# Attention passes of a graph network on one core: TensorE fetches one K|V row in 14 by one-hots kept in DRAM, and the weighed rows live in one buffer that is scanned in place

## The reference

```python
alpha = jnp.sum(q[dst] * k[src], axis=-1) * SCALE      # the third adds edge_bias[edge_type]
m = jax.ops.segment_max(alpha, dst, num_segments=N)
a = jnp.exp(alpha - m[dst])
denom = jax.ops.segment_sum(a, dst, num_segments=N)
out = jax.ops.segment_sum(v[src] * (a / denom[dst])[:, :, None], dst, num_segments=N)
```

## Time and profile before

| | us |
|---|---|
| median of 3 runs without a profile | 5822.36 (5817.04 to 5822.9) |
| the profiled execution (one), its span | 6562.2 |
| pass 2, 3 and 4 in it: from the first row fetch to the last | 1080, 1080, 1083 |
| pass 5 and 6 in it: from the first row fetch to the last | 1003, 992 |

### The profile page before, as it was taken

How to read it: one execution, slowest core, us unless ns; L and a number is a source line. 1 busy time by engine, 2 the same in 40 slices (tenths; PEclk the granted TensorE clock), 3 DMA queues, 4 the chain that set the end, 5 groups by cost and what they waited for, 6 DMA issues and landing times.

```text
span 6562.2 us, 44574 instructions
## 1 busy us (share of the span) xinstructions
PE 2310.6 (35%) x14635; PEld 1387.8 (21%) x14635; DVE 4507.3 (69%) x5353; ACT 2519.0 (38%) x3136; POOL 3944.3 (60%) x3878
## 2 busy tenths in 40 slices
PE   4988400000020000000100000046877783778886
PEld 2775300000000000000000000023444441444443
DVE  7978587777767777776787777764655653656654
ACT  2330144444424444443344444433444442444443
POOL 1001377777747777775677777656665555566664
PEclk8998755555555555555555555567888895889887
DMA  2233354444434444443454444412333322333332
GB/s 64 83 136 135 110 163 152 153 147 146 152 117 151 157 148 147 152 148 113 134 160 152 147 148 146 142 46 86 102 110 101 101 95 73 102 110 109 98 103 84
DMA packets 257146, 807.72 MB, mean 123 GB/s; under 512 B 72026, under 2 KB 108938, under 8 KB 253123
## 3 DMA queue, kind: packets, MB, share of 16 engines
q0 software_dynamic: 162688, 416.67, 22.2%
q1 hardware_dynamic: 94279, 389.14, 16.2%
HBM read 473.23 MB, written 332.30 MB: 123 GB/s over the span
## 4 chain that ended last, share of the span: by engine, by line
POOL 38%; PE 26%; issue 22%; DVE 8%; ACT 2%; another core or an unknown queue 2%; DMA 1%; SPq 0%; DVEq 0%; POOLq 0%; ACTq 0%
POOL arena L2316 38%; PE pair_ps L1864 20%; PE pair_ps L1966 3%; DVE outs L917 2%; ACT outs L1702 1%; PE banks_ps L1830 1%; PE banks_ps L1942 1%; DVE outs L995 1%; PE pair_ps L1873 0%; DVE bn_st L700 0%; DVE H L1048 0%; ACT arena L1680 0%; PE pair_ps L1982 0%; PE banks_ps L1807 0%
## 5 line engine op out<-in xcount | busy, mean ns | idle before, releaser
L2316 POOL DMA_INDIRECT arena<-table,src_i x3596 | 3684.6, 1025 | 1549.8 <-issue 1134.4
L1842 PE MATMUL pair_ps<-ident,tails 128*128 128x128 f32 x9 | 2.7, 439 | 3331.7 <-DVE tails L1246 3331.7
L1864 PE MATMUL pair_ps<-bias,arena 128*128 128x384 bf16 x4050 | 803.9, 348 | 279.9 <-issue 239.9
L1092 DVE TENSOR_TENSOR pair_ps<-pair_ps,arena 128x1792 f32<-128x1792 f32 x168 | 341.5, 2033 | 764.7 <-DMA arena<-table,src_i 589.1
L1864 PE MATMUL pair_ps<-work,arena 128*128 128x384 bf16 x4050 | 760.5, 338 | 206.4 <-issue 204.8
L995 DVE TENSOR_TENSOR_SCAN outs<-arena,banks_ps 128x1920 f32<-128x1920 f32 x112 | 465.2, 4153 | 494.3 <-ACT banks_ps L1688 446.2
L1842 PEld LDWEIGHTS pair_ps<-ident,tails 128*128 128x128 f32 x9 | 1.5, 213 | 3334.0 <-DVE tails L1246 3334.0
L1140 DVE TENSOR_TENSOR_SCAN work<-work,banks_ps 128x1920 f32<-128x1920 f32 x168 | 697.7, 4153 | 5.8
L1562 ACT ACTIVATE LD<-DE 128x112 f32<-128x112 f32 x168 | 49.8, 296 | 1440.9 <-issue 571.3
L1864 PEld LDWEIGHTS pair_ps<-bias,arena 128*128 128x128 bf16 x4050 | 406.9, 102 | 661.6 <-issue 452.8
L1582 ACT COPY outs<-work 128x1792 f32<-128x1792 f32 x171 | 541.0, 3165 | 0.0
(11 more groups left out here) (321 smaller groups left out, 4353.4 us busy)
## 6 DMA issues: line engine op xcount, KB each, us to landing
rows_att<-outs SPq DMA_DIRECT2D x165, 1008.0 KB
rows_plain<-outs SPq DMA_DIRECT2D x110, 896.0 KB
arena<-table,src_i POOLq DMA_INDIRECT x3596
kept_counts<-arena SPq DMA_DIRECT2D x15, 2000.0 KB, 6.4
bias<-sources SPq DMA_DIRECT2D x108, 192.0 KB
arena<-kept_counts SPq DMA_DIRECT2D x10, 2000.0 KB, 8.3
outs<-kept_counts SPq DMA_DIRECT2D x5, 2000.0 KB, 8.0
table<-arena SPq DMA_DIRECT2D x18, 512.0 KB, 3.0
```

Of the source, the lines that this page charges most:

```text
L1092: chain(v.tensor_tensor(prod, prod, ring[:, s, :, 0:D], ALU.mult))
L1864: ins = pe.matmul(picked_ps[g % 2], parts3[:, a, t, :], hots_made[g % 2][:, :, t, :], start=t == a == 0, stop=t == NB - 1 and a == 2)
L2316: pool.indirect_dma_start(dst, None, tab, bass.IndirectOffsetOnAxis(ap=idx, axis=0))\
```

## The change

Four things change in the attention passes.

1. From group 12 on POOL fetches 13 rows of a group, and PE makes the fourteenth: 25 tiles of the table times a one-hot of 125 x 128 bytes (fp8), for three bf16 parts of the table that add up to the f32 row, so 75 matmuls of 256 columns (`pick_table_row`). ACT copies the result from PSUM to the ring (`lay_pick`), and the product with K waits for that.
2. The table comes back from DRAM to SBUF at the start of each pass in 13 units of 2 tiles (`load_unit`), and DVE takes each apart into three bf16 parts with three casts and two subtractions (`split_units`), 5 units in group 0, 2 in group 1, and one each in groups 2 to 7. The parts stand where the edge bias and a node buffer stood; so the edge bias is stored to DRAM once and comes back by the group in pass 4.
3. The one-hots of the 44 groups are made once, ahead of the passes: SP clears 44 blocks of DRAM in the cells pass (`clear_hots`, 5 after each store of counts), POOL writes the ones by 44 indirect transfers of single bytes, and SP loads 400 KB per group in each pass (`load_hots`).
4. `OS` is one buffer, and the PSUM tile `msg` goes: the product of V with the weights writes `OS`, and the scan runs in place on it. The product waits until ACT has copied out the rows of the group before (it was two groups before). Clearing at the start of a pass gets shorter.

The core of the diff:

```diff
             def part_a(k, g):
...
+                split_units(k, g)
                 v.wait_ge(s_land[s], landed(k, g))
+                if row_picks(k, g):
+                    v.wait_ge(s_row_laid, row_pick(k, g) + 1)
                 chain(v.tensor_tensor(prod, prod, ring[:, s, :, 0:D], ALU.mult))
...
+            def split_units(k, g):
...
+                    for a in range(3):
+                        part = row_parts(k, a, t0, t1)
+                        ins = v.tensor_copy(part, rest)
+                        if a < 2:
+                            step(ins)
+                            step(v.tensor_tensor(rest, rest, part, ALU.subtract))
...
             def part_b(k, g):
...
-                chain(v.tensor_tensor(by_edge(msg).rearrange("p j (h c) -> p j h c", c=CH), vals, wts,
+                if g:
+                    v.wait_ge(s_rows, rows_base[k] + 2 * g)
+                chain(v.tensor_tensor(by_edge(OS).rearrange("p j (h c) -> p j h c", c=CH), vals, wts,
                                       ALU.mult))
-                if g >= 2:
-                    v.wait_ge(s_rows, rows_base[k] + 2 * (g - 1))
-                chain(v.tensor_tensor_scan(OS[b], dB[b], msg, 0.0, ALU.mult, ALU.add))
+                chain(v.tensor_tensor_scan(OS, dB[b], OS, 0.0, ALU.mult, ALU.add))
...
             def clear_carries(k, name):
-                step(v.memset(banks_ps[:, :], 0.0))
-                step(v.memset(work[:, 0:4 * GS], 0.0), f"cleared{k}")
+                step(v.memset(LA, 0.0))
+                step(v.memset(work[:, 0:3 * GS], 0.0), f"cleared{k}")
...
+            def lay_pick(k, s, b, n):
+                act.wait_ge(s_row_pick, n + 1)
+                act.copy(ring[:, s, GROUP - 1, :], row_ps[b]).then_inc(s_row_laid, 1)
...
             def near_pass(k):
...
                     lay_rows(k, g % RING, g % 2, g, stored(k, g))
+                    if ROW_FROM <= g + RING < GROUPS:
+                        lay_pick(k, g % RING, (g + RING) % 2, row_pick(k, g + RING))
...
+            def pick_table_row(k, g, it=None):
...
+                for t in range(NB):
+                    for a in range(3):
+                        ins = pe.matmul(row_ps[g % 2], hot[0:NX, t, :], row_parts(k, a, t, t + 1)[0:NX, 0, :],
+                                        start=t == a == 0, stop=t == NB - 1 and a == 2)
+                ins.then_inc(s_row_pick, 1)
...
             def store_rows(k):
...
+                        if ROW_FROM + 2 <= g + 5 < GROUPS:
+                            load_hots(k, g + 5)
...
+            def load_hots(k, g):
...
+                if g - 2 >= ROW_FROM:
+                    sp.wait_ge(s_row_pick, row_pick(k, g - 2) + 1)
...
-                        for j in range(GROUP):
+                        for j in range(GROUP - row_picks(k, g)):
                             fetch(ring[:, s, j, :], table[k], src_i[:, first + j:first + j + 1], s_land[s])
...
+            for h in range(ROW_PICKS):
+                pool.indirect_dma_start(row_hots, bass.IndirectOffsetOnAxis(ap=hot_at[:, h:h + 1], axis=0),
+                                        one_8[:, 0:1], None).then_inc(s_ones, 16)
```

More of the change, by code:

```diff
@@ L61 @@
 SHARE = 7
+ROW_FROM = 12
+ROW_PICKS = GROUPS - ROW_FROM
+UNIT = 2
+UNITS = -(-25 // UNIT)
+UNIT_BUF = 3
+UNITS_AT = (5, 2, 1, 1, 1, 1, 1, 1)
+HOT_ROWS = 1 << 12
+CLEAR_EACH = 5
 QROWS = SHARE + 1
@@ L350, in gnn_kernel, with row_parts @@
         columns_turned = work[0:PICKED // 2, columns_at:columns_at + 2 * P].rearrange("p (a e) -> p a e", a=2)
+        rows_in = {k: (KEEP[:, :] if k == 4 else H[:, :, :].rearrange("p i f -> p (i f)")).bitcast(BF16)
+                   .rearrange("p (i f) -> p i f", f=2 * D) for k in range(PASSES) if KINDS[k] == ATT}
+        more_rows = bias_flat[:, 0:(2 * NB - 1) * D].bitcast(BF16).rearrange("p (i f) -> p i f", f=2 * D)
+        odd_row = work[:, ODD_AT:ODD_AT + D].bitcast(BF16).rearrange("p (i f) -> p i f", f=2 * D)
+        def row_parts(k, a, t0, t1):
+            if a == 0:
+                return rows_in[k][:, t0:t1, :]
+            if a == 2 and t1 == NB:
+                return odd_row[:, t0 - (NB - 1):1, :]
+            return more_rows[:, (a - 1) * NB + t0:(a - 1) * NB + t1, :]
         HOT = NB * P // 2
@@ L1095, in part_a @@
                 if k == 4:
-                    chain(v.tensor_tensor(scores, scores, bias[:, first:first + GROUP, :], ALU.add))
+                    v.wait_ge(s_bias_in[g % BIAS_BUF], 16 * (g // BIAS_BUF + 1))
+                    chain(v.tensor_tensor(scores, scores, bias_in[:, g % BIAS_BUF, :, :], ALU.add))
                 chain(v.tensor_tensor_scan(flat(MS[:, s, :, :]), flat(fences[:, b, :, :]), flat(UA[:, b, 1, :, :]), 0.0,
@@ L1104, in part_a @@
                 assert n == A_STEPS[k]
+            def split_units(k, g):
+                if g >= len(UNITS_AT):
+                    return
+                if k == 2 and g == 0:
+                    v.wait_ge(s_bias_kept, 16)
+                for i in range(sum(UNITS_AT[:g]), sum(UNITS_AT[:g + 1])):
+                    t0, t1 = i * UNIT, min((i + 1) * UNIT, NB)
+                    rest = units[:, i % UNIT_BUF, 0:t1 - t0, :]
+                    v.wait_ge(s_unit[i % UNIT_BUF], units_loaded(k, i))
+                    for a in range(3):
[4 more added lines that the diff above has]
+                            step(v.tensor_tensor(rest, rest, part, ALU.subtract))
+                    ins.then_inc(s_split, 1)
             def move_on(k, g):
@@ L1650, in far_pass @@
                 whole_sixes = (GROUPS - RING) // SIX
-                with act.Fori(0, whole_sixes) as it:
+                for g in range(ROW_FROM):
+                    far_group(g % RING, g % OUT, g, stored(k, g))
+                with act.Fori(ROW_FROM // SIX, whole_sixes) as it:
                     for i in range(SIX):
@@ L2172, in store_rows @@
                 dst = rows[KINDS[k]].rearrange("(p t) f -> p (t f)", t=STEPS)
+                if KINDS[k] == ATT:
+                    for b in range(NBLK - QBUF, NBLK):
+                        sp.wait_ge(s_kvq[b % QBUF], kvq_count(k, b))
+                    if k == 4:
+                        for g in range(BIAS_BUF):
+                            load_bias(g)
+                    for i in range(sum(UNITS_AT[:3])):
+                        load_unit(k, i)
                 if k in PICKS:
@@ L2327, in far_group @@
                 pool.nop(nofuse=True)
-                for j in range(GROUP):
+                for j in range(GROUP - (not isinstance(g, int) or row_picks(k, g))):
                     fetch(ring[:, s, j, :], table[k], near_idx[:, s, 0, j:j + 1], s_land[s])
@@ L2350, in run_pass @@
                 with pool.If(slow > 0):
-                    for g in range(RING):
-                        far_group(k, g, g)
-                    with pool.Fori(1, LOOPS) as it:
+                    for g in range(ROW_FROM):
+                        far_group(k, g % RING, g)
+                    with pool.Fori(ROW_FROM // RING, LOOPS) as it:
                         for s in range(RING):
```

129 lines of the change are left out of this document (114 added, 15 removed).

## The result

The changed kernel takes 6226.55 us (median of 4 runs, 6218.81 to 6230.12) where the kernel before takes 5822.31: 1.070 times as long (95% interval 1.068 to 1.071), so 404 us slower. 6250 was forecast, 428 slower, with a range of 5980 to 6350.

A forecast was written before the change was run, and what follows sets the result against it. POOL's row fetches, one every 1.25 us, were taken to bound the attention groups. 5822 - 165 (fewer fetches) + 539 (scan's hold) + 47 (L1113's hold) + 9 (splits) = 6252, said as 6250 us, range 5980 to 6350.

The forecast's parts named there:

- POOL as the bound, 1.25 us per fetch: Attention groups: POOL starts a row fetch every 1.25 us, 17.5 us per group, and DVE has about 2.7 us to spare.
- The longer profiled execution: Profile of the kernel before: 740 us longer than its runs, because recording stretches it; the changed kernel's profile should stretch likewise.
- 132 fetches fewer, -165 us: Attention passes: 44 groups in 3 passes lose one 1.25 us fetch each, 165 us less.
- The scan in place, +539 us: Long DVE scan, now with two SBUF inputs: holds one fetch 3.33 us in each of 162 groups, 539 us, bounds 445 to 640.
- The window move behind it, +47 us: L1113, after the scan: holds a later fetch 0.34 us in 139 groups, 47 us, bounds nothing to 80.
- The splits, +9 us: DVE's 78 subtractions that take the table apart: 0.55 of them catch a fetch, 9 us, bounds nothing to 40.
- What should cost nothing: PE's picks (8.1 to 16.3 us each), ACT's copies, loads, clears and ones: all hidden behind other work, no time added.
- The sum: Whole kernel: 5822 - 165 + 539 + 47 + 9 = 6252, said as 6250 us, 7% slower; this case reaches 6110 to 6350.
- Groups: Attention passes: groups of about 21 us before the twelfth and 19.6 to 20 after it.
- The scan that holds nothing (5660): Rival at the fetch starting inside the scan: it takes 0.95 us, so the gain stands alone, about 5660 us; 8%.
- The stall that is real (6000): Rival: 2.10 us fetches late in a pass also happen without the profiler, and the hold hides them; 6000 us, 9%.
- the late picked row (6700): Rival: load, pick and copy run one after another, 23 us per group; DVE waits 3.4 us in 132 groups; 6700, 8%.

The follow-up runs named there:

- the run with 8 pieces: The changed kernel with the in-place scan cut into 8 scans of 16 channels each, all inputs still in SBUF: 5831.12 us, 1.002 times before.

## Why the prediction was right, step by step

**POOL as the bound, 1.25 us per fetch.** Right. The kernel before, profiled again, has passes of 1000, 993 and 1008 us; 790 transfers behind the first at 1.25 us each are 987.5. (The working counted 783 fetches and left out the windows, which before and after have alike.)

**The longer profiled execution.** The half on which the sum rests was right: its 740 us were of that execution. That the five passes seemed to hold 750 us of excess, so all of it, was luck: against the second profile they held 660, and 90 lay outside of them. The other half, "a profile of the changed kernel should be longer than its own runs in the same way", was wrong: its span is 6217.1 us and its runs take 6219 to 6230. Such stretching is no property of the kernel; the second profile told.

**132 fetches fewer, -165 us.** Right; the version with the scan's input back in PSUM is 165 us below before, and its passes lose about that beyond the smaller holds.

**The scan in place, +539 us.** Right in kind, place and count (162), and 19 us too large: 3.21 us each make 520. The working put every fetch 0.67 us into the scan and its end 0.80 behind it. In the trace the held ones start 0.05 to 1.29 us into it, 0.76 on average, and end 0.75 behind it. That the 0.67 of the kernel before still served is in part luck: the product's extra 1.2 us, which the working didn't have, moves the scan by nearly a whole step of 1.25 us from fetch to fetch. The lower bound was 445, the upper 640.

**The window move behind it, +47 us.** Measured 60.4 us in the changed kernel. The same instruction cost 24.1 in before, which the working didn't take off, so the change adds 36.

**The splits, +9 us.** Measured 4 us, with the casts, which the working didn't count.

**What should cost nothing.** It did: PE's picks take about 10.7 us each by the windows of pass 3 below (107.00 us for 750 matmuls, ten picks), inside the 8.1 to 16.3 forecast and far within a group of 20; ACT's copy takes 0.36 us, and DVE never waits for it. Two things were missed. The product into SBUF became 1.2 us longer, which was hidden by DVE's wait for rows but weighs in the run with 8 pieces. And outside the attention passes' fetches the profiled execution is 15 us longer than the second one of before, 12 of it between passes 2 and 3 and between 3 and 4 (91.6 and 112.2 us against 85.7 and 106.2). About 7 of these 12 lie ahead of the pass's last scan: it ends 24.0 us after the start of the pass's last fetch, where it was 20.5. The other 5 lie behind it. The version with the input in PSUM has both parts as well, the scan in place alone only 2 us of them, so they don't come from the scan's inputs; which of the other parts of the change makes them wasn't tried.

**The sum.** All other fetches together took 9 us beyond 0.947 in before and 3 in the changed kernel, so -6. Then -165 + 520 + 36 + 4 - 6 + 15 = 404, which is what was measured. The sum on record has 430: its three holds are 35 us too large, and it lacks the 6 us less and the 15 us more. Its range was drawn too narrowly: with its own bounds of 80 for the move and 40 for the splits, the top is 6417 and not 6350.

**Groups.** About 21 us before the twelfth and 19.6 to 20 after were forecast. From scan to scan it is 21.4, 21.4 and 21.6 us on average in the first eleven groups of the three passes, and 20.0, 20.0 and 20.1 after them.

**The rivals.** The scan that holds nothing (5660) is refuted by 162 fetches, and by the two experiments that put the time at 6376 and 5652 with that one input moved. The Trainium skill's page "SBUF — State Buffer", section "Who interferes with whom", has the rule that a VectorE instruction with two SBUF inputs contends with a GpSimd instruction that reads SBUF, and an inference that making descriptors needs only the write side. The trace agrees with the rule for the issue of these transfers, which read their row numbers from SBUF, whatever the output: 520 us. The inference, taken to mean that such an instruction leaves them alone, doesn't hold for them; no run here has a transfer of POOL without row numbers. The stall that is real (6000) falls with the second profile of before, the late picked row (6700) with DVE's waits, none of which is for it.

## What to carry to other kernels

Where POOL issues indirect transfers without a break, look at the operands of each long VectorE instruction beside them: when a buffer moves from PSUM to SBUF and leaves the instruction no input in PSUM, a transfer that starts inside it stands until its end, though the instruction itself is no slower. Price it per transfer, as the rest of the instruction less what the issue covers anyway, times the instructions that meet one. If space forbids PSUM for the whole tile, half of it at a time is enough; if that can't be had either, cut the instruction in a few pieces, but not in so many that its own engine becomes the bound.

## What the runs showed of the hardware

- A fetch that starts inside a scan with two SBUF inputs ends 0.75 us behind it, wherever the scan's output goes. The reach ends with the instruction: a series of scans lets fetches through in between. The first 0.04 us are an exception: the 8 fetches of the changed kernel that start there take 0.95 as ever, and it is the scan that lasts longer, 4.20 to 4.23 us instead of 4.16.
- It isn't the scan alone. In the whole trace of the changed kernel 388 of POOL's indirect transfers start well inside a VectorE instruction that reads from SBUF alone (over 0.06 us behind its start, over 0.3 ahead of its end), and all are held; 1335 start so inside one with an input in PSUM, and none is. Two inputs aren't needed: a cast of `split_units`, with one input in SBUF and its output there too, holds as well. In pass 3 a fetch that starts 0.22 us into one ends 0.82 behind it:

```profile
2129.33 0.43 DVE L1186 CAST H<-work 128x512 bf16<-128x512 f32 x1
2129.55 1.03 POOL L2501 DMA_INDIRECT arena<-table,src_i  x1 [0.30 <-issue]
```

- A scan costs 0.66, 1.16, 2.16 and 4.16 us for 240, 480, 960 and 1920 columns: 2.08 ns per column and 0.16 us apiece.
- A VectorE product that writes SBUF at a stride of 15 numbers (60 bytes) takes 3.24 us where the same product takes 2.02 in order; to PSUM at that stride it took 2.03. The Trainium skill, "SBUF — State Buffer", section "Door 1: The DMA port swizzle", says that SBUF has lines of 16 bytes and that each access that crosses to another pays. The trace agrees: with 60 bytes from number to number the product takes 1.6 times as long.
- The picks raise PE's granted clock. Windows of pass 3 in the changed kernel, ahead of the first pick and among them (busy time of PE, PEld, DVE, ACT and POOL, then the granted clock, DMA share and GB/s):

```profile
2000.00:2200.00 200.00, 0.00 (x0) 0.00 (x0) 164.70 (x147) 70.43 (x97) 158.87 (x136) 0.50 0.46 145
2400.00:2600.00 200.00, 107.00 (x750) 84.39 (x750) 156.82 (x98) 86.72 (x122) 159.87 (x132) 0.76 0.50 163
```

With PE idle the clock is at 0.50, the lower of its two levels (1.2 GHz); with picks it is 0.76 on average, between the two.
